# Feed-forward quantisation: a constant's addition moved to ScalarE, a subtraction to GpSimd

## What is computed

```python
def fp4_quant_dequant(x):            # blocks of 16 along the last dim
    scale = max(max|x in block| / 6, 1e-12)
    xn = x / scale
    q = GRID[searchsorted(MID, |xn|)] * sign(xn) * scale    # GRID 0 .5 1 1.5 2 3 4 6
    return q
gate = fp4_quant_dequant(x) @ fp4_quant_dequant(w_gate).T
y    = fp4_quant_dequant(x) @ fp4_quant_dequant(w_up).T
h    = silu(gate) * y
out  = fp4_quant_dequant(h) @ fp4_quant_dequant(w_down).T
```

## Time and profile before

| | us |
|---|---|
| median of 3 runs | 1453.99 |
| lowest and highest | 1449.19, 1454.34 |
| the profiled execution, its own time | 1453.21 |
| its span, first to last instruction | 1451.5 |
| TensorE busy | 1112.3 (77%) |
| VectorE busy | 933.2 (64%) |
| ScalarE busy | 822.6 (57%) |
| GpSimd busy | 637.6 (44%) |

### The profile page before, as it was taken

How to read it: one execution, slowest core, us unless ns; L and a number is a source line. 1 busy time by engine, 2 the same in 40 slices (tenths; PEclk the granted TensorE clock), 3 DMA queues, 4 the chain that set the end, 5 groups by cost and what they waited for, 6 DMA issues and landing times.

```text
span 1451.5 us, 33719 instructions
## 1 busy us (share of the span) xinstructions
PE 1112.3 (77%) x11264; PEld 860.6 (59%) x11265; DVE 933.2 (64%) x1715; ACT 822.6 (57%) x1442; POOL 637.6 (44%) x921
## 2 busy tenths in 40 slices
PE   0577659999986776369999905899998736999991
PEld 0355536666653555259999902555555325999991
DVE  5799648888937896853333355888998485333333
ACT  0455336777764553246666652767767624666665
POOL 3322154344401221036776613666776302677661
PEclk9999859999997998669999966999999956999996
DMA  8100023322200000101111132343233010111115
GB/s 254 35 1 0 1 48 65 57 57 66 55 15 0 1 0 1 58 21 49 48 47 46 47 121 59 63 81 67 59 73 75 2 58 17 49 48 47 48 47 181
DMA packets 160689, 74.96 MB, mean 52 GB/s; under 512 B 125451, under 2 KB 152852, under 8 KB 160596
## 3 DMA queue, kind: packets, MB, share of 16 engines
q1 hardware_dynamic: 151508, 55.06, 15.8%
q0 software_dynamic: 9088, 18.63, 4.2%
HBM read 28.03 MB, written 15.73 MB: 30 GB/s over the span
## 4 chain that ended last, share of the span: by engine, by line
PE 55%; DVE 22%; issue 7%; ACT 5%; DMA 4%; SPq 3%; POOL 2%; DVEq 1%; ACTq 0%; POOLq 0%
PE PS L1011 18%; PE PS L1039 9%; PE PS L668 4%; DVE m L794 4%; PE PS L385 3%; SPq L896 3%; PE PS L376 3%; PE PS L634 3%; PE PS L596 2%; PE PS L650 2%; DVE sg L794 2%; ACT pt L1115 1%; DMA qT<-qs 1%; PE PS L689 1%; PE PS L676 1%
## 5 line engine op out<-in xcount | busy, mean ns | idle before, releaser
L1011 PE MATMUL PS<-xTs,pt 128*128 128x128 f32 x2272 | 280.5, 278 | 0.0
L1011 PEld LDWEIGHTS PS<-xTs,pt 128*128 128x128 f32 x2272 | 269.1, 195 | 0.0
L742 ACT ACTIVATE pt<-PS 128x768 f32<-128x768 f32 (+1 forms) x256 | 225.7, 915 | 49.6 <-PE PS L596 24.4
L1158 DVE TENSOR_TENSOR pt<-pt,PS 128x512 f32<-128x512 f32 x142 | 97.6, 688 | 233.5 <-PE PS L1011 180.1
L1285 POOL DMA_INDIRECT xs<-rows,src x142 | 137.6, 969 | 170.1 <-DVE src L1152 127.5
L1074 ACT ACTIVATE pt<-wgu 128x1024 f32 x142 | 149.9, 1057 | 91.0 <-issue 82.1
L1295 POOL DMA_INDIRECT outs<-ys,dst x142 | 139.9, 985 | 93.9 <-DVE ys L1173 86.8
L794 DVE TENSOR_REDUCE m<-PS 128x4 f32<-128x1024 f32 x128 | 153.2, 1221 | 27.4 <-PE PS L596 25.0
L1039 PE MATMUL PS<-wdn,pt 128*128 x1136 | 150.3, 275 | 1.2 <-DVE ys L1173 1.2
L794 DVE TENSOR_REDUCE sg<-PS 128x6 f32<-128x768 f32 x128 | 118.1, 954 | 32.8 <-PE PS L596 31.1
L1039 PEld LDWEIGHTS PS<-wdn,pt 128*128 128x128 f32 x1136 | 138.0, 192 | 1.5 <-issue 1.5
(11 more groups left out here) (240 smaller groups left out, 2168.8 us busy)
## 6 DMA issues: line engine op xcount, KB each, us to landing
pt<-outs SPq DMA_DIRECT2D x16, 512.0 KB, 4.9
rows<-qT SPq DMA_DIRECT2D x12, 256.0 KB, 2.2
xs<-rows,src POOLq DMA_INDIRECT x142, 2.5
outs<-ys,dst POOLq DMA_INDIRECT x142, 2.3
wgu<-in_L_ffn_w_gate SPq DMA_DIRECT2D x1, 2048.0 KB
wgu<-in_L_ffn_w_up SPq DMA_DIRECT2D x1, 2048.0 KB
wdn<-in_L_ffn_w_down SPq DMA_DIRECT2D x8, 256.0 KB
out<-X SPq DMA_DIRECT2D x8, 256.0 KB, 4.4
```

What stands on the lines that cost most here:

```text
L742: s.activation(k.pt[:, a % 4, :, 0:w], k.PS[:, self.bank:self.bank + 2, 0:w], ACT.Exp, scale=self.scale).then_inc(self.s_p, 1)
L1011: last = t.matmul(k.PS[:, 1 + 2 * p + w, c * P:(c + 1) * P], k.wst[:, 1 - p, w, c * P:(c + 1) * P], k.xTs[:, p, :], start=True, stop=True)
L1158: v.tensor_tensor(k.hs[:, p, :], k.sgs[:, p, :], k.PS[:, 2 + 2 * p, :], ALU.mult).then_inc(self.s_h, 1)
```

## The change

The constant BASE is added by ScalarE: after the Square, a second activation, Copy with BASE as bias, works in place on `mg`, and waits for the Square by a semaphore of its own (`s_bare`). What was L312 becomes a plain addition of `mg` and `xn` and is VectorE's only pass of the two; it now signals `s_rounded`. The subtraction mg - xn goes to GpSimd, in place on `mg`, once for the x part and once for the h part, each ahead of the product that reads it and with a wait in between.

```diff
-        self.s_sq = k.sem("ffn_squares")
+        self.s_bare, self.s_sq = k.sem("ffn_bare_squares"), k.sem("ffn_squares")
...
-                ch.run(v.scalar_tensor_tensor(xn, mg, BASE, xn, ALU.add, ALU.add))
-                v.scalar_tensor_tensor(mg, mg, BASE, xn, ALU.add, ALU.subtract).then_inc(self.s_rounded, 1)
-
-        self.walk(eng, fn, ch, 4)
+                v.tensor_tensor(xn, mg, xn, ALU.add).then_inc(self.s_rounded, 1)
+
+        self.walk(eng, fn, ch, 3)
...
             mg = k.fmg[p][:, c]
+            ch.run(g.tensor_tensor(mg, mg, k.fxn[p][:, c], ALU.subtract))
             return g.tensor_tensor(k.xhq[:, c].rearrange("p (n k) -> p n k", k=BLK), mg.rearrange("p (n k) -> p n k", k=BLK),
...
-        self.walk(eng, fn)
+        self.walk(eng, fn, ch, 2)
...
-                s.activation(k.fmg[p][:, c], k.fxn[p][:, c], ACT.Square, scale=BINADE ** 0.5).then_inc(self.s_sq, 1)
+                mg = k.fmg[p][:, c]
+                s.activation(mg, k.fxn[p][:, c], ACT.Square, scale=BINADE ** 0.5).then_inc(self.s_bare, 1)
+                eng.wait_ge(self.s_bare, q0 + z + 1)
+                s.activation(mg, mg, ACT.Copy, bias=BASE).then_inc(self.s_sq, 1)
```

## The result

| | before | after |
|---|---|---|
| median, us | 1454.16 of 4 runs | 1509.22 of 4 runs (1507.12 to 1511.92) |
| ratio of after to before | | 1.0386, 95% interval 1.0355 to 1.0416 |
| profiled execution, its own time | 1453.21 | 1507.12 |
| its span | 1451.5 | 1505.2 |

The change makes the kernel slower by 3.9%; 3.3% was forecast (1502 us), and the range of 1481 to 1530 holds the result. In the profiled executions the difference is 53.9 us, against a sum of 48.

The account below looks back on a forecast made before the run. The bound was taken to be a chain of dependent operations through VectorE, ScalarE and TensorE, not VectorE's busy share; two runs of 19.6 plus 4.3 us add 48 to 1453.2, giving 1502 us, range 1481 to 1530.

Parts of the forecast that it names:

- sum of 48: Whole kernel: two feed-forward runs, each 19.6 us for thirteen steps plus 4.3 at the ends, make it 48 us slower.
- The links: Feed-forward step: operations each starting as the one before ends, through VectorE, ScalarE and TensorE, set its 7.34 us.
- The Copy, 1.05 less 0.2 of slack: ScalarE's queue, ahead of the hqT copies: the added pass costs 1.05 us, 0.2 of it free, so 0.85 a step.
- The subtractions, 0.68 and 1.54: GpSimd: one for the x part, 0.68 us, one for h, 1.54; its work per step grows from 1.96 to 4.3.
- Scale and xn find GpSimd in the way: VectorE's scale and xn passes wait out GpSimd operations through mutual exclusion; the step was taken as 9.0 us.
- both ways: Scale gets in between GpSimd's operations, xn ends at 8.7 us; or scale is too late, xn ends at 9.5.
- the first way: Scale gets in behind GpSimd's h subtraction, xn waits for the h product: 8.7 us; the 9.0 taken lies nearer to it.
- TensorE's clock: Feed-forward up and y products: no slowdown in the forecast; a rival had them at most double at a lowered clock.
- the second rival: TensorE idles some 2.4 us a step and loses its clock every second step: 10.0 us on average, 1526 us; 13%.
- Start and end of a run: First x part and first full scale cost 1.1 us, the last h-only groups 3.2: together 4.3 us a run.
- Rival 3: VectorE's queue is the bound and time does not rise: 1450 us, or 1439 with a cheaper Copy; 5%.
- the sum's own bounds: Whole kernel: from the bounds of the subtractions, steps of 8.5 to 9.8 us, 34 to 69 us more, 1487 to 1522.

Follow-up runs that it names:

- copy_only: Kernel after with the subtraction given back to VectorE as a second pass; ScalarE's Copy kept, GpSimd only the products: 1.0225 of the kernel before, 1481.74 us.
- x_on_pool: Kernel before with late statistics and early Square, no Copy; GpSimd also adds the constant and subtracts for the x part alone: 0.9963 of before, 1447.55 us.
- reorder_after: Kernel after with statistics behind the forming of h, Square and Copy ahead of the normalisation, GpSimd's h part first: 1.0432 of the kernel before, 1516.65 us.
- sub_only: Kernel after without ScalarE's Copy (constant 0, rounding left out), subtractions kept on GpSimd: 1.0192 of the kernel before, 1478.78 us.
- after_bn_late: Kernel after with VectorE's two statistics passes moved behind the forming of h, so scale need not wait for X: 1.0213 of the kernel before, 1481.03 us.

## Why the prediction was right, and where not

- **The links, not the busy shares.** Right. VectorE lost 20.6 of 72.6 busy microseconds in the stretch and the time rose. L313 was no link: with it VectorE waits 0.18 us for X in `copy_only`, without it 1.38 in the kernel after. No run takes L313 away by itself.
- **The Copy, 1.05 less 0.2 of slack.** Right. The row is 1.00, starts about 0.04 after the Square, and the step of `copy_only` is about 0.85 longer once scale's own wait is taken off. hqT comes 2.83 us behind xn's end instead of 1.79, 1.04 more where 1.05 was expected. Two small errors cancel: the slack gave back 0.30, not 0.2, and y takes 2.06 instead of 1.95. One thing was left out: GpSimd's products do not run beside VectorE's reduction alone, they end at 93.02, in the scale pass, and with the Copy they hold scale up by another 0.1 to 0.2.
- **The subtractions, 0.68 and 1.54.** A little low: 0.73 and 1.67. GpSimd's chain of a step is 4.5 (109.53 to 114.05), not 4.3.
- **Scale and xn find GpSimd in the way.** Right in both ways, and in size: 9.0 less 7.34 and 0.85 left 0.81 for it, and 0.73 was measured in the loop. That the first way would be the more frequent also held, in two steps of three.
- **TensorE's clock.** This is the step that failed: the sum put it at nothing. As reasons against the second rival the prediction named that "with transposes inside the wait TensorE is idle for less than half of the step", and that the clock had held at 78% busy. But the wait is in one piece: the x transposes come right behind y (111.10) and are over at 111.53, and the h transposes then wait for GpSimd's last product (2.51 us at 95.47, 2.65 at 114.18). From 104.95 on the clock fell to 0.50 in one step of three, not in every second one, and then cost about 0.9 us. It also fell at the start of each run. In the first, TensorE waits 6.32 us until 58.85, the clock is 0.50 from 56 to 64 (0.71 before) and again from 70 to 72 (1.00 before), and the two steps there took 5.6 us more where 3.0 was forecast. So the second rival's mechanism is part of the outcome. With 0.91 in the 80 us it stayed above the 0.9 that the prediction had set for it, but over all thirteen steps the clock is 0.87 in the first run and 0.89 in the second (before 0.97 and 0.96). By the rule that the prediction took from the Trainium skill, page "TensorE: Matmul & The Clock Gate", section "HAM oscillation — how this bites in real kernels", the rate falls again and again; the rows agree with that in some steps, not in each: after 2.65 us empty at 114.18 it stayed at 1.00.
- **Start and end of a run.** Together 3.6 and 4.4, forecast 4.3. The start was priced too high, the end a little too low.
- **Rival 3** is excluded for this order: no step inside the loop was under 8.2.

The 5.9 us by which the sum missed the profiled difference are thus the steps: 25.08 and 22.85 for 19.6 each, 8.7 in all, mostly the clock and the two first steps, less 0.6 at the ends and 2.2 in later phases that the change does not touch. Why those differ stays open; repeated runs of one kernel spread by more than that. The result lies inside the sum's own bounds (1487 to 1522) too, but not for their reason: they allowed for longer subtractions and for scale coming too late, and the excess is mostly the clock.

## What to carry to other kernels

Follow one step through all engines before you move work off the busiest one: here VectorE was 91% busy, and a pass less was worth nothing, as the step waited for ScalarE's queue and, through it, for X. Work for GpSimd has two prices, the VectorE passes that it shuts out and the time at which its last result lets TensorE go on; the second can take TensorE's clock with it. Before moving work, try to move waits: three changes of order, with the same instructions, gave 1.4%, where moving the work cost 3.9%.

## What the runs showed of the hardware

- The exclusion acts in both directions, and the waiting counts as part of the instruction that waits. xn took 2.27 us instead of 1.16 behind a GpSimd product (`x_on_pool`), and GpSimd's subtraction of 256 columns 1.64 instead of 0.73 behind xn (`reorder_after`). An xn of 960 columns that had to wait ends 1.01 or 1.02 us after that GpSimd operation (kernel after, `sub_only`, `after_bn_late`, `reorder_after`, `x_on_pool`).
- It depends on what GpSimd does: xn took 1.16 beside a fill and 2.00 beside a subtraction at the same place. Scale was held up by fills too, 1.53 instead of 0.22.
- A VectorE pass that already waits gets in when one GpSimd operation ends and the next is due. Scale did so in a gap of 0.08 us (112.59 to 112.67), and xn in `reorder_after` with no gap in the rows: the h product ends at 104.44, the next subtraction starts at 104.40 and then waits for xn. Between two fills issued back to back scale did not get in.
- A subtraction of two full tensors on GpSimd takes 1.67 us for 704 columns, the product with a broadcast scale 1.39: the shape alone does not give the price.
- TensorE's granted clock was 0.50 after a wait of 2.66 us (h transposes at 86.38) and one of 2.51 (95.47), yet 1.00 after one of 2.65 (114.18). The length of the wait alone does not decide it; what else does was not tried.
